# Early first group norm, constants as rows turned by TensorE, and a convolution that starts ahead of the last stores

## The reference

```python
def _gn(v, G=32, eps=1e-5):
    g = v.reshape(B_, G, C_ // G, H_, W_)
    m = jnp.mean(g, axis=(2, 3, 4), keepdims=True)
    s = jnp.var(g, axis=(2, 3, 4), keepdims=True)
    return ((g - m) / jnp.sqrt(s + eps)).reshape(v.shape)

x = x + layer0(_gn(x))
x = x + layer1(_gn(x))
```

## Time and profile before

| what | value |
|---|---|
| median of three runs | 2846.17 us |
| the profiled execution, its own time | 2843.61 us |
| its span in the trace | 2841.6 us |
| TensorE (PE) busy | 2570.7 us, 90% |
| VectorE (DVE) busy | 2524.0 us, 89% |
| ScalarE (ACT) busy | 1482.7 us, 52% |
| GpSimd (POOL) busy | 84.9 us, 3% |
| mean granted clock of TensorE | 0.984 |

### The profile page before, as it was taken

The page is one execution under the profiler, slowest core; times in us unless marked ns, Lnnn a source line. Parts: engine busy times, 40 slices in busy tenths (PEclk is TensorE's granted clock), DMA queues, the critical chain, the costliest instruction groups (busy, mean ns, idle before and its releaser), DMA issues. The chain is left out here.

```text
span 2841.6 us, 50920 instructions
## 1 busy us (share of the span) xinstructions
PE 2570.7 (90%) x17291; PEld 1867.2 (66%) x17291; DVE 2524.0 (89%) x3511; ACT 1482.7 (52%) x1920; POOL 84.9 (3%) x155
## 2 busy tenths in 40 slices
PE   0039999999999999999999699998599999999998
PEld 0026666666666666666666466666499999999997
DVE  7968999999999999999999799998788888888884
ACT  0033354555545555555323277777466666666663
POOL 0020000000000000000000100000200000000000
PEclk9999999999999999999999799999799999999999
DMA  8966112332323223322100499997999999999996
GB/s 331 416 213 178 61 35 81 107 94 74 87 91 106 78 80 104 97 74 84 42 17 1 150 366 369 365 369 290 245 279 291 288 290 291 294 302 288 290 287 185
DMA packets 346041, 546.38 MB, mean 192 GB/s; under 512 B 133536, under 2 KB 244896, under 8 KB 345888
## 3 DMA queue, kind: packets, MB, share of 16 engines
q1 hardware_dynamic: 321984, 465.80, 52.2%
q10 hardware_dynamic: 23424, 77.08, 8.0%
q0 software_dynamic: 480, 1.51, 0.2%
HBM read 363.88 MB, written 180.44 MB: 192 GB/s over the span
## 5 line engine op out<-in xcount | busy, mean ns | idle before, releaser
L774 PE MATMUL qk_qb<-qk_xhi,whi 128*128 128x384 f16 x2592 | 846.5, 327 | 20.0 <-DVE qk_xlo L670 14.3
L774 PE MATMUL qk_qb<-qk_xlo,whi 128*128 128x384 f16 x2592 | 846.4, 327 | 0.0
L774 PE MATMUL qk_qb<-qk_xhi,wlo 128*128 128x384 f16 x2592 | 846.2, 326 | 0.0
L691 DVE SCALAR_TENSOR_TENSOR qk_dw<-qk_pool,qk_wd,qk_dw 128x768 f32<-128x768 f32 (+2 forms) x864 | 837.6, 1010 | 0.6 <-ACT qk_dw L543 0.6
L678 DVE TENSOR_REDUCE qk_pool<-qk_qb 128x192 f32<-128x768 f32 x432 | 412.1, 954 | 67.2 <-PE qk_qb L774 50.5
L774 PEld LDWEIGHTS qk_qb<-qk_xhi,whi 128*128 128x128 f16 x2592 | 254.0, 98 | 183.3 <-DVE qk_xlo L670 17.5
L1675 PE MATMUL cv_cb<-cv_hi,cv_toep 128*128 128x288 f16 x1536 | 347.9, 287 | 27.7 <-DVE cv_lo_last L1607 22.4
L774 PEld LDWEIGHTS qk_qb<-qk_xhi,wlo 128*128 128x128 f16 x2592 | 254.0, 98 | 168.4 <-issue 1.4
L774 PEld LDWEIGHTS qk_qb<-qk_xlo,whi 128*128 128x128 f16 x2592 | 254.0, 98 | 162.8 <-issue 1.0
L1681 PE MATMUL cv_cb<-cv_hi_next,cv_toep 128*128 128x288 f16 x1536 | 346.5, 287 | 0.0
L1550 ACT ACTIVATE cv_res<-cv_cb,cv_cst 128x288 f32<-128x288 f32 x384 | 187.5, 502 | 299.7 <-PE cv_cb L1681 238.0
(11 more groups left out here) (182 smaller groups left out, 3534.7 us busy)
## 6 DMA issues: line engine op xcount, KB each, us to landing
cv_toep<-toeplitz_scratch SPq DMA_DIRECT2D x384, 256.0 KB, 7.0
cv_raw<-patch_scratch SPq DMA_DIRECT2D x192, 325.0 KB, 7.6
st_x<-in_x SPq DMA_DIRECT2D x24, 2304.0 KB, 17.1
qk_xf<-in_x SPq DMA_DIRECT2D x72, 768.0 KB, 4.2
pr_xb<-in_x SPq DMA_DIRECT2D x24, 2304.0 KB, 12.0
out<-cv_rows ACTq DMA_DIRECT2D x72, 768.0 KB, 7.1
patch_scratch<-pr_turned SPq DMA_DIRECT2D x39, 832.0 KB, 11.2
patch_scratch<-cv_raw SPq DMA_DIRECT2D x36, 832.0 KB, 11.4
```

What stands on the lines that cost most here:

```text
L691: V.scalar_tensor_tensor(acc, pool[:, o, r + y:r + y + n, x:x + PW], wd[:, o, k:k + 1], acc, ALU.mult, ALU.add).then_inc(taps_done, 1)
L774: ins = nc.tensor.matmul(qbank[s % NQB][:, h, 0:2 * W], w[:, b, o * P:(o + 1) * P], x[:, par, j // 2, b, at_row:at_row + 2 * W], start=n = ...
```

## The change

It has three parts. In the statistics stage SP loads chunks alone. The weights and constants are issued from ScalarE's queue once the first chunk is used; the fourteen vectors come as rows of 128 numbers (54 rows in all), one transpose on TensorE turns them, and ScalarE copies them out. VectorE's preparation of weights and kernels moves from behind chunk 4 to behind chunk 12.

The first group norm is computed about an early average `base`, taken from the means of the first 20 chunks while the last four are still read. `group_affine` is gone: behind the last chunk VectorE sums deviations from `base`, their squares and the records' squares, the stage ends, and one set of seven products (only neighbouring blocks share a group) averages both sums at the head of `stage_qkv`. The first two chunks are then normalised, rounded and subtracted in pieces of 768 pixels, shared between ScalarE and VectorE, and a slot waits for its own half chunk alone. The second chunk has its own buffer, which lies in `dw`; POOL clears `dw` only behind the last piece. TensorE runs 24 products whose result is not used.

The convolution's first loads are issued behind the last store of block 0, ahead of those of blocks 1 and 2. The last stores are waited for later, at channel 8 of the first group. POOL's middle rows of blocks 1 and 2 wait for the first four channels. TensorE runs 48 transposes at the head of the stage, and the averages of the second group norm take seven products instead of nine.

```diff
         def _(sp):
             for i in range(XBUFS):
                 sp.dma_start(xs[:, i], src[:, :, i * CHUNK:(i + 1) * CHUNK]).then_inc(x_in[i], 16)
-            sp.dma_start(wst[:, :, :], wT.rearrange("(b p) n -> p b n", p=P)).then_inc(w_in, 16)
-            sp.dma_start(kern[:, :, :, :], w_large.rearrange("(b p) o y x -> p b (o y) x", p=P)).then_inc(c_in, 16)
-            sp.dma_start(ws[:, :, :, :], w_small.rearrange("(b p) o y x -> p b (o y) x", p=P)).then_inc(c_in, 16)
-            for n, a in enumerate(norms):
-                sp.dma_start(bn[:, n, :], a.rearrange("(b p) -> p b", p=P), allow_slow_non_contiguous=True).then_inc(c_in, 16)
-            ahead.constants(sp)
             with sp.Fori(1, STEPS // XBUFS) as r:
                 for i in range(XBUFS):
                     address(sp, (r * XBUFS + i) * CHUNK)
...
         def _(act):
+            act.wait_ge(x_used, 1)
+            vectors = [*norms, ahead.b_qkv, ahead.b_dw]
...
+            for a in vectors:
+                n = a.shape[0] // P
+                act.dma_start(rows[row:row + n, :], a.rearrange("(b p) -> b p", p=P)).then_inc(rows_in, 16)
+                row = row + n
+            act.dma_start(wst[:, :, :], wT.rearrange("(b p) n -> p b n", p=P)).then_inc(w_in, 16)
+            act.dma_start(kern[:, :, :, :], w_large.rearrange("(b p) o y x -> p b (o y) x", p=P)).then_inc(c_in, 16)
+            act.dma_start(ws[:, :, :, :], w_small.rearrange("(b p) o y x -> p b (o y) x", p=P)).then_inc(c_in, 16)
+            ahead.constants(act)
+            act.wait_ge(turned_consts, 1)
+            nc.scalar.activation(bn[:, :, :].rearrange("p n b -> p (n b)"), turn[:, 0:NBN], ACT.Copy).then_inc(bn_ready, 1)
+            nc.scalar.activation(ahead.bq[:, :], turn[:, NBN:NBN + QO], ACT.Copy)
+            nc.scalar.activation(ahead.bd[:, :], turn[:, NBN + QO:NBN + 2 * QO], ACT.Copy)
             act.wait_ge(w_in, 16)
             nc.scalar.activation(whi[:, :, :], wst[:, :, :], ACT.Copy, scale=SCALE).then_inc(whi_ready, 1)
...
             statistics(0)
+            with dve.Fori(1, ROUNDS // 2) as r:
+                statistics(r)
             dve.wait_ge(whi_ready, 1)
             V.scalar_tensor_tensor(wlo[:, :, :].rearrange("p b n -> p (b n)"), wst[:, :, :].rearrange("p b n -> p (b n)"),
                                    SCALE, whi[:, :, :].rearrange("p b n -> p (b n)"), ALU.mult, ALU.subtract)
-            dve.wait_ge(c_in, 16 * 14)
+            dve.wait_ge(c_in, 16 * 2)
+            dve.wait_ge(bn_ready, 1)
...
-            with dve.Fori(1, STEPS // XBUFS) as r:
+            with dve.Fori(ROUNDS // 2, ROUNDS - 1) as r:
                 statistics(r)
...
+            dve.wait_ge(x_used, (ROUNDS - 1) * XBUFS)
+            V.tensor_reduce(sums[:, :], records[:, :, 0:KNOWN, 1], AX.X, ALU.add).then_inc(sums_ready, 1)
+            statistics(ROUNDS - 1)
+
+            dve.wait_ge(guess_done, 1)
+            chained(V.tensor_scalar(base[:, :], guess[:, 0:CB], 1.0 / KNOWN, None, ALU.mult))
+            dve.wait_ge(x_used, STEPS)
...
+            V.tensor_reduce(part[:, 0], records[:, :, :, 2], AX.X, ALU.add)
+            V.tensor_reduce(cols[:, :, 0], dev[:, 0], AX.X, ALU.add)
+            chained(V.tensor_reduce(part[:, 1], dev[:, 1], AX.X, ALU.add))
+            V.scalar_tensor_tensor(cols[:, :, 1], part[:, 0], 2.0 / 512, part[:, 1], ALU.mult, ALU.add)
+
+        @block.tensor
+        def _(pe):
+            pe.wait_ge(made, 3 + 2 * CB)
+            pe.wait_ge(rows_in, 16 * 14)
+            nc.tensor.transpose(turn[:, 0:NBN + 2 * QO], rows[:, :],
+                                ident[0:NBN + 2 * QO, 0:NBN + 2 * QO]).then_inc(turned_consts, 1)
+            pe.wait_ge(sums_ready, 1)
+            for o in range(CB):
+                near = [b for b in range(CB) if abs(b - o) <= 1]
+                for b in near:
+                    ins = nc.tensor.matmul(guess[:, o:o + 1], member[:, b, o * P:(o + 1) * P], sums[:, b:b + 1],
+                                           start=b == near[0], stop=b == near[-1])
+            ins.then_inc(guess_done, 1)
...
             for b in range(CB):
-                load(1, b)
+                start.load_into(sp, second[:, b], 1, b, x2_in[b])
             for b in range(CB):
-                load(2, b)
+                sp.wait_ge(lo_half, b + 1)
+                sp.wait_ge(lo_ready, b + 1)
+                start.load(sp, 2, b)
             sp.wait_ge(blank_made, 1)
             sp.wait_ge(late_zero, 1)
...
+            def early_norm(n, b):
+
+                early_loaded(act, n, b)
+                nc.scalar.activation(early(n, b), early(n, b), ACT.Identity,
+                                     bias=bx[:, b:b + 1], scale=sx[:, b:b + 1]).then_inc(act_norm, 1)
+
+            def early_high(n, b):
+
+                h, k = PIECES[n]
+                early_normed(act, n, b)
+                nc.scalar.activation(xhi[:, 0, h, b, k * HALVES:(k + 1) * HALVES], early(n, b),
+                                     ACT.Copy).then_inc(hi_half if k == 0 else hi_ready, 1)
...
+            nc.scalar.activation(root[:, :], var[:, :], ACT.Sqrt, bias=eps[:, :], scale=UNSCALE).then_inc(root_ready, 1)
             act.wait_ge(prep, 2)
-            act.wait_ge(c_in, 16 * (3 + 2 + len(TOPK)))
-            for h in range(HALF):
+            act.wait_ge(c_in, 16 * (1 + 2 + len(TOPK)))
+            for n in range(2 * HALF):
                 for b in range(CB):
-                    norm(h, b)
-                    high(h, 0, h, b)
+                    if (n, b) in BY_ACT:
+                        early_norm(n, b)
+                for b in range(CB):
+                    early_high(n, b)
             for b in range(CB):
                 norm(HALF, b)
...
+            gp.wait_ge(lo_half, HALF * CB)
+            gp.wait_ge(lo_ready, HALF * CB)
             G.memset(dw[:, :, 0:PW], 0.0).then_inc(zeroed, 1)
             G.memset(padw[:, :, :, :, :], 0.0).then_inc(pad_made, 1)
...
+            V.scalar_tensor_tensor(var[:, :], averages[:, 1:2 * CB:2], 1.0 / RECORDS, sq[:, :],
+                                   ALU.mult, ALU.subtract).then_inc(var_ready, 1)
+            V.tensor_tensor(mean[:, :], base[:, :], off[:, :], ALU.add).then_inc(link, 1)
+            dve.wait_ge(root_ready, 1)
+            V.reciprocal(sx[:, :], root[:, :]).then_inc(prep, 1)
             dve.wait_ge(prep, 1)
+            dve.wait_ge(link, 3)
             V.scalar_tensor_tensor(bx[:, :], mean[:, :], -1.0, sx[:, :], ALU.mult, ALU.mult).then_inc(prep, 1)
...
+            def early_norm(n, b):
+
+                early_loaded(dve, n, b)
+                V.tensor_scalar(early(n, b), early(n, b), sx[:, b:b + 1], bx[:, b:b + 1], ALU.mult, ALU.add).then_inc(dve_norm, 1)
+
+            def early_low(n, b):
+
+                h, k = PIECES[n]
+                early_normed(dve, n, b)
+                if k == 0:
+                    dve.wait_ge(hi_half, h * CB + b + 1)
+                else:
+                    dve.wait_ge(hi_ready, h * CB + b + 1)
+                window = slice(k * HALVES, (k + 1) * HALVES)
+                V.tensor_tensor(xlo[:, 0, h, b, window], early(n, b), xhi[:, 0, h, b, window],
+                                ALU.subtract).then_inc(lo_half if k == 0 else lo_ready, 1)
...
-            for h in range(HALF):
+            early_norm(0, 1)
+            early_norm(1, 1)
+            early_norm(1, 2)
+            for b in range(CB):
+                early_low(0, b)
+            early_norm(2, 1)
+            for b in range(CB):
+                early_low(1, b)
+            early_norm(3, 1)
+            early_norm(3, 2)
+            for n in range(2, 2 * HALF):
                 for b in range(CB):
-                    low(h, 0, h, b)
+                    early_low(n, b)
...
+            WARM = 24
...
+            for o in range(CB):
...
+                    ins = nc.tensor.matmul(averages[:, 2 * o:2 * o + 2], member[:, b, o * P:(o + 1) * P], cols[:, b, :],
+                                           start=b == near[0], stop=b == near[-1])
+            ins.then_inc(avg_done, 1)
+            for n in range(WARM):
+                nc.tensor.matmul(qbank[1][:, 0, 0:2 * W], whi[:, 0, 0:P], whi[:, 0, 0:2 * W],
+                                 start=n == 0, stop=n == WARM - 1)
...
+                        if at(t, 0) and s < JPO and s % 2 == 0:
+                            pe.wait_ge(lo_half, s // 2 * CB + CB)
+                        elif at(t, 0) and s < JPO:
+                            pe.wait_ge(lo_ready, s // 2 * CB + CB)
+                        elif s < JPO and s % 2 == 0:
...
@@ -1088,14 +1182,14 @@
                 sp.wait_ge(tr_out, STEPS * NRUN + (b + 1) * RPB)
                 sp.dma_start(patch_dram[:, STEPS, b * (P // GRP):(b + 1) * (P // GRP), :].rearrange("p g n -> p (g n)"),
                              turned[STEPS % 2][:, b].rearrange("p c j -> p (c j)")).then_inc(stored[STEPS % 2][b], 16)
-            sp.wait_ge(stored[0][0], 16 * (STEPS // 2 + 1))
```

(21 more changed lines are left out.)

140 lines of the change are left out of this document (70 added, 70 removed).

## The result

The changed kernel takes 2819.45 us (median of 4, 2817.09 to 2820.00) against 2845.44 for the kernel before on the same chip: ratio 0.9909, 95% interval 0.9897 to 0.9922. On another chip it took 2819.35 against 2844.44, ratio 0.9914 (0.9900 to 0.9927). The forecast was 2818.0. Its profiled execution took 2820.0, with a span of 2818.3, 23.3 us shorter than before. The second chip's run had been expected at 2817 to 2820 us.

A forecast was written before the change was run, and what follows sets the result against it. Time can be won only where TensorE waits: before its first products and between projection and convolution. Head -17.2 and convolution -10.0 make -27.2 us, giving 2816.4 from the profiled run, 2819.0 from the median; forecast 2818, range 2809 to 2831.

The forecast's parts named there:

- Statistics: Statistics stage: without the hole behind chunk 4, the sums begin at about 156.9 instead of 163.24, 6.3 us earlier.
- The condition: Statistics stage: constants get in among the chunks by a generous deadline, issued by about 30 and needed at 82.
- The norm's chain: First group norm, from sums to scales: 8.0 us instead of 18.1, scales ready at 164.9 instead of 181.35.
- The first pieces: Head of qkv: pieces done 16.0 us after the scales, slot 2 at 181.9, TensorE 21.0 us ahead.
- Chunk 3: Qkv stage: its late load, behind the blank stores, stalls TensorE about 4 us near 240; head worth 17.2, not 21.0.
- The convolution's start: Head of the convolution: TensorE starts 10.6 us earlier; the whole is worth 10.0 us, between 4 and 14.5.
- The 2.9 us: Convolution's start: VectorE's slowing under POOL's copying and sends, said to be moved by the later copies, not saved.
- The 7.1: Convolution's start: worth 7.1 us instead of 10 if VectorE's 2.9 fall on pieces for which TensorE waits.
- Rival B: Convolution's start is bound by the DMA and gives only 4 us; 21.2 go in all, 2824; chance 0.15.
- The sum: Whole kernel: -17.2 for the head and -10.0 for the convolution, -27.2 us together; forecast 2818.
- Rival A: Qkv head: chunk 3 is no hindrance, so 21.0 + 10.0 = 31.0 us go, 2814; chance 0.14.
- D: Qkv head: POOL's chain, stretched by VectorE, takes 41 instead of 7.4; blank stores at 222, kernel 2852; chance 0.03.

The follow-up runs named there:

- vectors by number: The changed kernel with its fourteen vectors read one number for each partition from ScalarE's queue, without transpose or copies out: 2844.66 us, ratio 1.0001.
- rows left out: The changed kernel with blank stores behind chunk 3, and POOL's middle-row copies and sends for blocks 1 and 2 left out: 2810.93 us, ratio 0.9882.
- moved stores: The changed kernel with the nine blank stores issued behind the three loads of chunk 3 instead of ahead of them: 2814.12 us, ratio 0.9898.
- POOL in group 1: The changed kernel with POOL's middle rows of blocks 1 and 2 made after 28 channels, in the second group, instead of 4: 2817.43 us, ratio 0.9906.
- POOL at once: The changed kernel with blank stores behind chunk 3 and POOL's wait for the first four channels taken out: 2813.32 us, ratio 0.9892.

## Why the prediction was right, and where it was not

**Statistics.** Forecast 156.9 for the sums; 156.94. The preparation of 7.8 was 8.0. That the sum is exact is luck: the weights and constants among the chunks cost 7.2 us for 5.5, and the last twelve chunks took 5.36 each back to back instead of 5.44, 1.0 less in all, with smaller differences beside them. The condition was weaker than stated: I had the constants issued by about 30 and needed at 82, and they were issued at 56.2. The run with vectors by number shows what this depended on. There the seven vectors issued from 23.78 to 65.05 took 5.90 us each. Spread over 16 engines a vector of 384 numbers is 24 for each engine, so 0.246 us a number, and at the 401 GB/s of this stretch one engine moves 6.2 KB in that time: one row of a chunk (1536 numbers of 4 bytes, 6144 B). So by my estimate each number waits for one row of a chunk. The Trainium skill, DMA: Bandwidth & Descriptors, "Queues, rings and completion order", says that engines take turns between queues packet by packet; the trace agrees (up to 110 us the profile counts 6400 packets for the chunks' 37.75 MB, about a row each), and I drew half of the consequence. Turns by packet protected the queue of large packets, 0.4 to 1.0 us for a chunk, and starved the one of small packets, 5.9 us for a vector.

**The norm's chain.** 8.0 forecast for the sums to the scales, 8.3 measured (165.28). The five instructions took 0.59 to 0.72 each, not 0.51.

**The first pieces.** 182.37 against 181.9: right. TensorE's lead at slot 2 is 20.6, for 21.0.

**Chunk 3.** Blank stores at 188.86 (188.4), the tap at 241.41 (241.1), ScalarE's wait 17.7 (17), one gap of 4.0 (about 4) near 240: the mechanism held. The step that failed is the sum's last one, "TensorE two slots later. How much slack lies between is in rows 7", and its 17.2. The gap was the right size, but TensorE met it in front of ScalarE's emptying of the transposes and not of the maxima, and the sum had no term for what the gap does to the clock. It fell to 0.92 and 0.74 in two stretches of 10 us, and cost 2.8 us more, nearly all in the second (10 busy us at 0.74 are 2.6). 20.6 - 4.0 - 2.8 is 13.8; the marker shows 13.6, and 20.7 with the gap removed. The forecast for the head was 17.2.

**The convolution's start.** 10.0 forecast, 10.2 measured, but two sizes within it were wrong and cancel, which is luck. TensorE did not wait for the first matrices, issued 12.0 us earlier than the head alone gives instead of 7.8: the sends went out 7.8 earlier as forecast, and the first matrices 5.8 behind them instead of 10.0. It waited for VectorE, and started 13.5 earlier for 10.6. Of that it gave back 3.3 for the forecast's 0.6. VectorE's normalisations under POOL's copies took 3.75 instead of 1.88, and TensorE waited 6.7 us. That is where the Trainium skill's rule on the port that VectorE and GpSimd share (SBUF — State Buffer, on who interferes with whom) had it. The 2.9 us that I took as the price fit the whole first quarter before, whose later rows were longer too; the row shown gives 1.9 of them. The 7.1 did not come true, since TensorE started 2.9 earlier than forecast. Nor can the price be saved alone: with POOL's copies moved away, TensorE waited 3.1 us for VectorE and 3.8 for matrices instead of 9.9 for ScalarE. Rival B is not the first limit, but with the rows left out the waits for matrices are 3.1 us.

**The sum.** 27.2 forecast; 23.3 in the profiled execution (13.1 and 10.2), 26.0 and 25.1 between medians. The profiled execution of after was the slowest of its four. The head gave 13.1 to 13.6 for 17.2, and nothing in the trace makes up for these 4 us: that the median came within 1.5 us of 2818 is in part the choice of executions. From the profiled execution before, the same sum gives 2816.4, and the one after took 2820.0. Rival A (no hindrance by chunk 3) was excluded by the gap, and is what the moved stores give. D did not occur: POOL's chain took 7.3 us.

**The faster version.** With the blank stores behind chunk 3, with or without POOL's wait, the kernel takes 2814.1 and 2813.3 (ratios 0.9898 and 0.9892), below both kernels. The intervals of both overlap that of the change, but the marker stands at 287.71 to 288.86 in all four profiles that have the stores moved, 4.1 to 7.1 us ahead of the change's two, 292.94 and 294.81.

## What to carry to other kernels

When a wait is removed, look at what stands behind the next wait in the same queue, and not only at who uses its data: an early normalisation that nobody needed yet held up the emptying of a PSUM bank. Add to each gap of TensorE the time at the lower granted clock behind it; here 4.0 us cost 6.8, and 2.2 us cost 4.1. A second DMA queue helped constants past bulk loads here only when they came in few, large packets.

## What was not expected of the hardware

- Two DMA queues share the engines by packets, not bytes: beside a queue of 6144-byte rows, a vector of 384 single numbers took 5.6 us to issue, where most took 0.5 before.
- POOL's memset and its issuing of transfers seem to slow VectorE as its copies do: four normalisations took 3.90 us at 1983.89 beside the memset (until 1985.65) and the issuing of two sends (until 1988.4), and 1.88 without POOL. No run takes either away.
- Four arrangements of the convolution's start (the change, POOL in group 1, POOL at once, 48 transposes left out) end within the 1253.5 to 1256.3 of the seven profiles with the change's own convolution, though TensorE's start differs by 3.6 us and its waits by up to 6. The waits show VectorE, ScalarE and the matrices taking turns as its limit; which of them sets the sum was not isolated.
